# FFN blocks of batches 0 to 2 moved half a step to a step earlier in a fused selective-scan and FFN kernel, and one C product of the last step moved from GpSimd to VectorE

## The reference

```python
u  = silu(causal_conv4(in_proj_w @ ctx) + conv_b)            # (b, 512 channels, 512 positions)
dt_low, B, C = split(x_proj_w @ u)                           # ranks 16, 16, 16
dt = softplus(dt_proj_w @ dt_low + dt_proj_b)
state_t = state_{t-1} * exp(dt_t * A) + (dt_t * u_t) * B_t   # 16 states per channel
y  = sum_n state * C + D * u
x  = x + (y * silu(layernorm(x))).T
x  = x + layernorm(x) @ sum_r(factors[r]) / sqrt(8) + bias
```

## Time and profile before

| | us |
|---|---|
| median of 3 runs | 506.89 |
| lowest and highest run | 505.04, 507.24 |
| the profiled execution's own time | 503.0 |
| its span in the trace | 501.2 |
| busy: DVE / POOL / PE / ACT | 469.0 / 453.0 / 431.6 / 346.5 |

### The profile page before, as it was taken

One profiled execution on the slowest core, in us unless ns is written; L12 is line 12 of the kernel. 1 busy time (PEld: TensorE's weight loads), 2 busy tenths in 40 slices (PEclk: granted clock), 3 DMA queues, 4 the chain that ended last, 5 costly groups with the idle time before them and its releaser, 6 DMA issues.

```text
span 501.2 us, 4086 instructions
## 1 busy us (share of the span) xinstructions
PE 431.6 (86%) x1028; PEld 179.7 (36%) x1036; DVE 469.0 (94%) x368; ACT 346.5 (69%) x620; POOL 453.0 (90%) x237
## 2 busy tenths in 40 slices
...
GB/s 185 250 368 335 185 84 116 88 41 233 329 276 56 0 1 0 63 1 27 332 339 43 1 21 1 21 1 0 166 397 157 1 21 21 32 11 21 1 0 84
DMA packets 17871, 53.96 MB, mean 108 GB/s; under 512 B 2724, under 2 KB 3236, under 8 KB 16824
## 3 DMA queue, kind: packets, MB, share of 16 engines
...
...
## 4 chain that ended last, share of the span: by engine, by line
POOL 36%; PE 21%; DVE 19%; issue 17%; ACT 4%; DMA 1%; SPq 0%; POOLq 0%; DVEq 0%; ACTq 0%
POOL h L1104 24%; PE y L509 10%; POOL h L1097 9%; DVE dA L953 9%; DVE h L959 3%; DVE h L953 3%; PE work L486 2%; POOL dtu L1090 2%; PE work L409 2%; ACT dA L774 2%; DVE acc L910 1%; PE work L502 1%; PE work L429 1%; DMA w_in<-w_inT 1%; PE work L436 1%
## 5 line engine op out<-in xcount | busy, mean ns | idle before, releaser
L1104 POOL TENSOR_TENSOR h<-b_rep,dtu 128x1024 f32<-128x1024 f32 x127 | 301.8, 2441 | 12.5 <-DMA b_rep<-bc_scratch 11.2
L509 PE MATMUL y<-h,ident 128*128 128x512 f32 x508 | 248.4, 627 | 37.2 <-DVE h L959 35.0
L774 ACT ACTIVATE dA<-dt,a_neg 128x512 f32<-128x512 f32 x256 | 165.7, 679 | 85.1 <-DVE h L959 74.9
L953 DVE TENSOR_TENSOR_SCAN dA<-dA,h 128x1024 f32<-128x1024 f32 x83 | 189.7, 2285 | 4.8 <-ACT dA L774 4.8
L509 PEld LDWEIGHTS y<-h,ident 128*128 128x128 f32 x508 | 96.3, 198 | 173.9 <-issue 108.6
L1097 POOL TENSOR_TENSOR h<-h,c_rep 128x1024 f32<-128x1024 f32 x45 | 107.1, 2382 | 11.8 <-DVE h L953 11.7
L953 DVE TENSOR_TENSOR_SCAN h<-dA,h 128x1024 f32<-128x1024 f32 x45 | 102.5, 2280 | 4.5 <-ACT dA L774 4.5
L959 DVE TENSOR_TENSOR h<-dA,c_rep 128x1024 f32<-128x1024 f32 x82 | 99.8, 1217 | 1.2
L409 PE MATMUL work<-ctx_sb,w_in 128*128 128x512 f32 x60 | 35.0, 716 | 15.1 <-DVE x L995 14.3
L502 PE MATMUL work<-fsum,xnT 128*128 128x512 f32 x64 | 29.2, 598 | 0.0
L910 DVE SCALAR_TENSOR_TENSOR acc<-work,chan,acc 128x511 f32<-128x511 f32 (+2 forms) x30 | 21.7, 731 | 5.3 <-ACT acc L641 5.0
...
## 6 DMA issues: line engine op xcount, KB each, us to landing
...
```

What stands on the lines that cost most here:

```text
L509: mm = pe.matmul(y[:], ident[:], h[:, (s * PAIRS + j) % H_RING, i, :], start=False, stop=(j == sum_order(s)[-1] and i == 1))
L774: act.activation(dA[:, j % 2, i, :], dt[:, k % 2, :], ACT.Exp, scale=a_neg[:, k, 2 * j + i:2 * j + i + 1]).then_inc(exp_done, 1)
L953: dve.tensor_tensor_scan(pair if on_pool(s * PAIRS + j) else decay, decay, pair, 0.0, ALU.mult, ALU.add).then_inc(scanned, 1)
L1104: pool.tensor_tensor(h[:, (s * PAIRS + j) % H_RING], b_rep[:, j], dtu[:, k % 2, :].unsqueeze(1).to_broadcast([P, 2, L]), ALU.mult).then_in ...
```

## The change

It moves work in the written order of the engines, and moves one product between two engines. No shape changes.

- Blocks 1 to 7: MEAN, VAR and NORM one slot earlier; TURN from slot 0 of step t+5 to slot 6 of step t+4; EVAC from slot 4 of step t+5 to slot 0 of it; LAYER from the head of step t+6 to the head of step t+5 (blocks 4 to 6 alike; block 7 had its own places); FINAL one step earlier. Block 0 keeps MEAN, VAR, NORM, TURN and EVAC, and has LAYER at slot 3 and FINAL at slot 7 of step 5.
- The copy of the factors' means moves on ACT from slot 7 to slot 4 of step 4; `centre` moves from four slots of step 5 to two of step 4 and two of step 5; scaling from slots 4 to 7 of step 5 to slots 0 to 3.
- Statistics, layer, bias and final sums of blocks 8 to 11 move earlier by up to a step. Blocks 12 to 15 start one to two slots earlier on PE, and one matmul of block 15 is made in the last step.
- In the last step j = 5 is no longer among POOL's C products.

```diff
-SCALE_SLOTS = (4, 5, 6, 7)
-CENTRE_SLOTS = (2, 4, 5, 6)
+SCALE_SLOTS = (0, 1, 2, 3)
+CENTRE_SLOTS = ((4, 6), (4, 7), (5, 0), (5, 1))
-RAW_STATS = {8: ((12, 5), (12, 6), (12, 7)), 9: ((13, 0), (13, 1), (13, 1)),
-             10: ((13, 2), (13, 3), (13, 3)), 11: ((13, 4), (13, 5), (13, 5))}
-RAW_LAYER = {8: (13, -1), 9: (13, 2), 10: (13, 6), 11: (14, 1)}
-RAW_FINAL = {8: (13, 2), 9: (13, 5), 10: (14, 0), 11: (14, 4)}
-RAW_BIAS = {8: (13, 1), 9: (13, 3), 10: (13, 6), 11: (14, 1)}
+RAW_STATS = {8: ((12, 3), (12, 4), (12, 4)), 9: ((12, 5), (12, 6), (12, 6)),
+             10: ((12, 7), (13, 0), (13, 0)), 11: ((13, 2), (13, 2), (13, 3))}
+RAW_LAYER = {8: (12, 5), 9: (13, -1), 10: (13, 3), 11: (14, -1)}
+RAW_FINAL = {8: (13, 0), 9: (13, 2), 10: (13, 6), 11: (14, 2)}
+RAW_BIAS = {8: (12, 7), 9: (13, 1), 10: (13, 3), 11: (13, 6)}
-LAST_POOL_C = (0, 2, 4, 5)
+LAST_POOL_C = (0, 2, 4)
-LAST_SUM_ORDER = (1, 0, 3, 2, 4, 6, 5, 7)
+LAST_SUM_ORDER = (1, 0, 3, 2, 5, 4, 6, 7)
...
-            early = {t: ((t + KB, 5), (t + KB, 6), (t + KB, 7), (t + KB + 1, 0), (t + KB + 1, 4),
-                         (t + KB + 2, -1), (t + KB + 2, 2)) for t in range(2 * KB)}
-            early[2 * KB - 1] = early[2 * KB - 1][:LAYER] + ((3 * KB, 5), (3 * KB + 1, 0))
+            early = {t: ((t + KB, 4), (t + KB, 5), (t + KB, 6), (t + KB, 6), (t + KB + 1, 0), (t + KB + 1, -1),
+                         (t + KB + 1, 2)) for t in range(2 * KB)}
+            early[0] = ((KB, 5), (KB, 6), (KB, 7), (KB + 1, 0), (KB + 1, 4), (KB + 1, 3), (KB + 1, 7))
...
-                    if i in (1, 4) and s < STEPS - 1:
+                    if i in (1 + k % 2, 4) and s < STEPS - 1:
                         for w in w_at(s)[i // 4:i // 4 + 1]:
                             turn_w(s, w)
...
-                    if s == STEPS - 2 and i == 5:
+                    if s == STEPS - 2 and i == 3:
                         pe.wait_ge(d_dt, STEPS)
                         z_layer(0, (0, 1))
-                    if s == STEPS - 2 and i == 6:
+                    if s == STEPS - 2 and i == 5:
                         pe.wait_ge(r_final, KB)
                         z_layer(1, (0, 1))
...
+                    if s == STEPS - 1 and i == 6:
+                        pe.wait_ge(mulc, dve_products(STEPS * PAIRS - 2))
+                        z_layer(3, (0,))
...
-                    if s == KB and j == 7:
+                    if s == KB and j == 4:
                         act.wait_ge(f_mean, 1)
                         act.activation(row_b[:], work1[:], ACT.Copy).then_inc(f_mean_evac, 1)
...
-                    if s == KB + 1 and j in CENTRE_SLOTS:
-                        centre(CENTRE_SLOTS.index(j))
+                    if (s, j) in CENTRE_SLOTS:
+                        centre(CENTRE_SLOTS.index((s, j)))
```

More of the change, by code:

```diff
@@ L499, in last_layer @@
             def last_layer(t):
+                if t == 0:
+                    pe.wait_ge(f_scaled, KB)
+                    pe.wait_ge(bias_split, 3)
                 pe.wait_ge(t_xnT, t + 1)
@@ L583, in step @@
                         z_layer(2, (0, 1, 2))
-                    if s == STEPS - 1 and i == 2:
+                    if s == STEPS - 1 and i == 3:
                         z_layer(0, (2,))
                         z_layer(1, (2,))
+                    if s == STEPS - 1 and i == 6:
+                        pe.wait_ge(mulc, dve_products(STEPS * PAIRS - 2))
+                        z_layer(3, (0,))
                     if i == 5 and new_batch:
@@ L618, in _ @@
             for s in range(STEPS):
-                if s == KB + 2:
-                    pe.wait_ge(f_scaled, KB)
-                    pe.wait_ge(bias_split, 3)
                 step(s)
-            pe.wait_ge(mulc, dve_products(STEPS * PAIRS - 2))
-            z_layer(3, (0,))
+            z_layer(3, (1,))
             for half in range(2):
@@ L628, in _ @@
                 if t == KB - 1:
-                    z_layer(t, (1, 2))
+                    z_layer(t, (2,))
                 pe.wait_ge(z_late, t // 2 + 1)
@@ L828, in step @@
                         var_sum(g_mv, b + 1, k, g_scratch, g_mean, s + 1, g_var)
-                    if j in (2 if s == STEPS - 1 else 4 if s > 3 * KB else 5, 7):
+                    if j in (2 if s == STEPS - 1 else 4 if s in (3 * KB, STEPS - 2) else 5, 7):
                         for w in w_at(s)[j // 7:j // 7 + 1]:
```

2 lines of the change are left out of this document (1 added, 1 removed).

## The result

The changed kernel takes 513.26 us, median of 4 runs (512.09 to 518.75), against 505.97 us for the kernel before on the same chip (4 runs, 503.52 to 507.24): ratio 1.018, 95% interval [1.013, 1.024]: slower, though the interval leaves open whether by more or by less than 2%. 513.6 was forecast. The profiled execution is the longest of the four, 518.75 us.

What follows compares the result with a forecast made beforehand. DVE's idle time was taken as the bound. Terms 4.5 + 2.0 + 3.4 + 0.1 (steps 7 to 10) + 1.8 + 1.9 - 5.9 - 1.1 = +6.7 us, added to the median 506.89, gave 513.6 us; range 503.8 to 517.

Steps and rivals of the forecast that it cites:

- Step 4, the copy: Scan (4, 5): its decays stand behind ACT's copy, which waits for PE's means; DVE loses 4.5 us, bounds 4.2 and 4.8.
- Steps 4 and 5, POOL: POOL's first subtraction waits for the copy; scans (5, 0) and (5, 1) wait 1.2 and 0.7; +2.0 us, bounds 0 and 3.
- Steps 5 and 6, PE behind: Block 0's LAYER in step 5 delays PE, TURN and EVAC; scan (6, 1) waits 2.5; +3.4 us, bounds 1.5 and 4.5.
- Steps 4 to 6 together: The copy, POOL and PE-behind terms of steps 4 to 6 taken together: +9.9 us.
- Step 11: Late TURN and EVAC delay scan (11, 1) by 1.5; NORM and statistics cost 0.3 in (11, 6); +1.8 us, bounds 0 and 2.5.
- Step 12: Block 8's MEAN, VAR and NORM ahead of ACT's other work: 1.1 at scan (12, 4), 0.75 at (12, 5); +1.9 us.
- Step 13: DVE's four waits, 6.75 us, go except 0.8 for block 10's matmuls; -5.9 us, bounds 3 and 6.75 won.
- The end: Gate of step 14 gives 1.4 back, the moved C product costs nothing, block 15's matmuls win +0.3; -1.1 us.
- (2): Rival: only the copy's wait in step 4 is real, later leads hold; 503.5 us, faster; chance 0.2.
- (3): Rival: copy and POOL cost their 6.5 us, the heads of the steps nothing; 506.4 us, same; chance 0.12.
- (4): Rival: PE's clock falls in steps 4 and 5, doubling a LAYER, 4 us more; 517.5 us; chance 0.1.
- The late terms: The terms for steps 11 to 15 taken together: -3.3 us.

Runs made afterwards that it cites:

- e1: Kernel before with only the means' copy at slot 4 of step 4 and the subtractions and scaling moved as in the change; 512.76 us, ratio 1.013.
- e9: The changed kernel measured again, nothing edited; 515.95 us, ratio 1.019 to the kernel before.
- e6: Kernel before with only the change's end: blocks 12 to 15 earlier, j = 5 of the last step on DVE; 503.88 us, ratio 0.996.
- e7: Kernel before with only blocks 5 to 7 moved as in the change, TURN at slot 5, block 4 as transition; 504.74 us, ratio 0.997.
- e2: Changed kernel with PE's means one place earlier in step 4, ahead of the sum of (4, 3); 509.63 us, ratio 1.008 to the kernel before.
- e3: Changed kernel with TURN of blocks 1 to 7 one slot earlier, at slot 5; 514.04 us, ratio 1.017 to the kernel before.
- e10: Changed kernel with means earlier on PE, copy at slot 5, subtractions in step 5, TURN at slot 5, new late tables kept; 506.03 us, ratio 1.001.
- e11: Kernel of e10 but late tables as before, except `raw_final` of block 9 at (13, 6); step 14's z layers as in the change; 502.68 us, ratio 0.994.
- e4: Changed kernel with the late tables of blocks 8 to 11 and blocks 12 and 13 in step 14 as before; 511.48 us, ratio 1.014.
- e5: Changed kernel with `raw_final` of block 10 one slot later, slot 7 of step 13; 512.09 us, ratio 1.012 to the kernel before.

## Why the prediction was right, and where it was not

The direction, the main mechanism and the time (513.6 forecast; 513.26 and 515.95 in two sets) were right. Steps 11 and 13 were not, and the total is as near as it is by luck in part: errors of opposite sign cancel in it, and two executions of the same kernel differ by as much as these errors.

- **Step 4, the copy (+4.5): right.** The wait is 5.18 in e1 and e9. The kernel before had lost 1.32 at scan (4, 4), just ahead of it, where e1 and e9 lose 0.56; the 0.76 less there comes back here, 5.18 - 0.76 = 4.4. Those 1.32 us belong to the profiled execution and not to the kernel, however. Scan (4, 4) in the kernel before and in e6, with the same instructions up to there:

```profile
157.21 2.29 DVE L953 TENSOR_TENSOR_SCAN h<-dA,h 128x1024 f32<-128x1024 f32 x1 [1.32 <-ACT dA L774]
```

```profile
158.84 2.29 DVE L955 TENSOR_TENSOR_SCAN h<-dA,h 128x1024 f32<-128x1024 f32 x1 [0.56 <-ACT dA L776]
```

Against e6 and e7 the copy costs 5.2. PE's sum of (4, 3), from which the means follow, starts 14.48 us after scan (4, 0) in the kernel before, 14.46 in e1 and 14.45 in e9: the input had not moved, as assumed, and e2 showed by moving it that it alone set the price.

- **Steps 4 and 5, POOL (+2.0): right.** 1.28 and 0.62 in e1 where 1.2 and 0.7 were forecast, POOL's wait 8.23 where 8.4 was. Steps 4 and 5 of e1 grew by 6.6 together, forecast 6.5.
- **Steps 5 and 6, PE behind (+3.4): mechanism right, too large.** Scan (6, 1) waited 1.24, not 2.5, and step 6 grew by 1.84; e3 and e7 show that the LAYER in the second half of a step is what costs, and TURN's place only which scan pays. (The working has a slip besides: 198.3 + 6.5 + 4.5 is 209.3, not 209.1.) The term was mis-sized where it kept 3.65 us for `in_proj`. It waited for DVE and had an idle time of 2.87 before; it takes 1.95 after an idle time of 0.37 in the changed kernel. The low clock had moved, not vanished: the second half of step 5 has a granted clock of 0.75 instead of 0.88, but `in_proj` is outside the low part. PE's timeline and the window of the changed kernel, then `in_proj` in e6, which has the instructions of before:

```profile
196.91 1.95 PE L409 MATMUL work<-ctx_sb,w_in 128*128 128x512 f32 x4 [0.37 <-DVE x L997]
...
185.70:199.40 13.70, 10.36 (x24) 4.97 (x25) 13.56 (x11) 8.74 (x18) 13.70 (x6) 0.75 0.00 1
```

```profile
186.51 1.95 PE L409 MATMUL work<-ctx_sb,w_in 128*128 128x512 f32 x4 [1.35 <-DVE x L997]
```

So neither duration belongs to one of the two orders; the 3.65 was what one execution of before had. In e10 and e11, where `in_proj` of the new order takes 3.65 and 3.60, step 6 is 32.21, 3.3 more than before: with the duration that the working kept, its 3.4 is what comes out (there with TURN at slot 5). At full clock it was to be 1.5, its lower bound, and 1.84 came.

- **Steps 4 to 6 together**: forecast +9.9, measured +10.0, of which 1.6 is the one sum at half clock; +8.4 in e9.
- **Step 11 (+1.8): too small.** +3.62, and +3.08 in e9. Scan (11, 1) waited 2.45 where 2.2 were expected; scans (11, 6) and (11, 7) another 1.65 where 0.3 were. With TURN one slot earlier (e3) those two waits are gone, so TURN's place is needed for them, which the working did not follow. But it takes the new tables as well: in e4, with TURN's place of the changed kernel and the old tables, they are gone too.
- **Step 12 (+1.9): right.** +2.10; scan (12, 4) waited 2.20 and (12, 5) 0.74, where 2.0 and 0.75 were forecast. e4 and e10 show that these are the new late tables' price.
- **Step 13 (-5.9): this failed.** Measured -2.76 for step 13 and -0.65 for step 14 (one `raw_final` of 0.75 us moved from one to the other). The working had 0.8 us of wait left for block 10; 2.43 were left (2.28 in e9), and e5 shows that `RAW_FINAL` stands too early for them. PE in step 13 of the changed kernel:

```profile
435.31 3.06 PE L512 MATMUL y<-h,ident 128*128 128x512 f32 x4 [2.64 <-DVE h L961]
438.16 1.06 PE L468 MATMUL work<-ident,x 128*128 128x128 f32 x4
439.15 1.27 PE L436 MATMUL work<-dt_low,w_dt 32*128 32x512 f32 x2
440.36 1.98 PE L512 MATMUL y<-h,ident 128*128 128x512 f32 x4
442.18 3.60 PE L478 MATMUL work<-fsum,x 128*128 128x512 f32 x8
```

PE itself waits 2.64 for DVE's product, runs its sum partly at half clock, then `turn_w` (L468) and `dt_proj` (L436) and one more sum before block 10's matmuls (L478). What gain there was belongs in the main to blocks 6 and 7 (e4, e7), not to the tables.

- **And the 3.40 us of the earlier trace rows was itself partly chance.** The same instructions in e6 and e1, which leave step 13 as it was, gave 2.15 and 2.31 us and a step of 33.79 where the profiled execution of before had 35.24. First PE in the kernel before, then PE and DVE in e6, ahead of the matmuls of block 9:

```profile
417.53 3.44 PE L509 MATMUL y<-h,ident 128*128 128x512 f32 x4
```

```profile
420.85 1.98 PE L509 MATMUL y<-h,ident 128*128 128x512 f32 x4 [0.21 <-DVE h L961]
...
427.55 0.75 DVE L944 SCALAR_TENSOR_TENSOR x<-work,t_r,x 128x512 f32<-128x512 f32 x1 [2.15 <-PE work L478]
```

Against 33.79 the changed kernel's step 13 gains 1.3 to 2.5, not 2.8 to 3.9. A wait taken from one execution was counted as fully there to be won.

- **The end (-1.1): right as far as it can be told.** The timings of e6 give 1.8 us, its interval from 0.3 to 3.4; the last step of the changed kernel is 0.26 shorter in one execution and 1.68 in the other. Of the 1.4 us that the gate of step 14 was to give back, e6 has all 1.54, but the changed kernel only 0.5 (a wait of 1.03) and 0.8 (0.78 in e9); why is open.
- **The rivals.** (2) and (3) fell with steps 5, 6, 11 and 12. (4), PE's clock, was there as one sum at half clock in one execution of two, 1.6 us, and a granted clock of 0.75; e9's shorter execution has that same 0.75 (its 181.6 to 195.3 us), so it did not decide the time. The doubled LAYER that this rival was priced by did not come: the large part of block 0's LAYER took 3.60 in step 5 of the changed kernel.

The late terms (steps 11 to 15) came out at +2.1 instead of -3.3, or -1.1 in e9. The sum had +6.7; the medians grew by 7.3 and 10.1 us in the two sets, and e9's execution by 7.34 from scan (4, 0) on. It is that near because errors cancel: step 6 counted 1.6 too high, step 11 1.3 to 1.8 too low, steps 13 and 14 too favourable by 1.3 to 2.5.

What stays open: how much of the late tables' loss of 3.5 us lies in step 13 and how much in PE's clock, since only one execution of e10 was profiled. What is said of single steps rests on one profiled execution of each kernel; of the parts' shares the timings alone settle only that of step 4 (e1).
